# The convolution's input in another order in memory: tile-major, with stepped reads on TensorE

## What is computed

```python
x = x + 0.5 * ffn(layernorm(x))            # ffn: fft over channels, sparse complex weight, ifft, + bias
h = layernorm(layernorm(x), norm1_w, norm1_b)
y = causal_conv_over_time(h, K) + D * h    # K[c, t] = sum_n mix[c, n] * exp(-tau[n] * dt * t)
v = layernorm(x) + y
v = v + gelu(layernorm(v, norm2_w, norm2_b) @ fc1.T + fc1_b) @ fc2.T + fc2_b
x = x + v
x = x + 0.5 * ffn(layernorm(x))
```

## Time and profile before

| | |
|---|---|
| median of 3 runs | 2264.78 us (2264.18 to 2265.57) |
| profiled execution | 2266.64 us, its span 2264.9 us |
| busy share of the span | PE 91%, DVE 59%, ACT 34%, POOL 26% |
| chain that ended last | PE 76%, DVE 8%, POOL 5%, issue 5%, ACT 2% |
| first u written | from 115.6 us |
| first state matmul | 488.51 us |
| MLP's first transposes | 691.82 us |
| largest groups | L1546 678.3 us, L1567 665.6 us (both PE, the MLP) |

### The profile page before, as it was taken

The page is one execution under the profiler, slowest core; times in us unless marked ns, Lnnn a source line. Parts: engine busy times, 40 slices in busy tenths (PEclk is TensorE's granted clock), DMA queues, the critical chain, the costliest instruction groups (busy, mean ns, idle before and its releaser), DMA issues.

```text
span 2264.9 us, 28385 instructions
## 1 busy us (share of the span) xinstructions
PE 2054.4 (91%) x10640; PEld 1034.3 (46%) x10640; DVE 1334.3 (59%) x2099; ACT 766.9 (34%) x939; POOL 596.4 (26%) x416
## 2 busy tenths in 40 slices
PE   7976766639887999999999999999999999999998
PEld 6433323227663444444444444444444444444443
DVE  4899999987787273562726436273562726537242
ACT  1476676756563131221312213031230312213020
POOL 0177777755442021120201102021120211202001
PEclk9988898869897999999999999999999999999999
DMA  6243222138894001101011010101101011010000
GB/s 233 98 177 153 74 88 97 38 88 237 256 274 132 20 30 45 38 19 38 20 56 38 20 38 19 49 28 36 38 19 38 19 56 38 19 38 19 19 19 19
DMA packets 96119, 157.45 MB, mean 70 GB/s; under 512 B 7426, under 2 KB 41730, under 8 KB 95235
## 3 DMA queue, kind: packets, MB, share of 16 engines
q1 hardware_dynamic: 96004, 155.77, 20.9%
HBM read 100.69 MB, written 63.41 MB: 72 GB/s over the span
## 4 chain that ended last, share of the span: by engine, by line
PE 76%; DVE 8%; POOL 5%; issue 5%; ACT 2%; DMA 1%; SPq 1%; DVEq 0%; POOLq 0%; ACTq 0%
PE psum L1546 29%; PE psum L1567 29%; PE psum L1418 9%; PE psum L1410 3%; POOL taps L556 2%; DVE arena L1057 2%; PE psum L1472 2%; POOL taps L553 2%; POOL va L525 1%; ACT arena L704 1%; PE psum L1381 1%; PE psum L1463 1%; DVE ring L1150 1%; PE psum L1392 1%; PE psum L1399 1%
## 5 line engine op out<-in xcount | busy, mean ns | idle before, releaser
L1546 PE MATMUL psum<-arena 128*128 128x512 f16 x3072 | 678.3, 380 | 1.6 <-DVE arena L1267 1.5
L1567 PE MATMUL psum<-arena 128*128 128x512 f16 x3072 | 665.6, 379 | 0.0
L799 ACT ACTIVATE arena<-psum,b1p,sc 128x512 f32<-128x512 f32 x256 | 199.5, 779 | 1037.4 <-PE psum L1546 1037.4
L1567 PEld LDWEIGHTS psum<-arena 128*128 128x128 f16 x3072 | 300.6, 98 | 362.3
L1546 PEld LDWEIGHTS psum<-arena 128*128 128x128 f16 x3072 | 300.9, 98 | 353.4 <-issue 7.5
L525 POOL TENSOR_TENSOR va<-va,mhalf 128x4 f32<-128x4 f32 x80 | 108.8, 1364 | 1295.6 <-DVE va L919 1244.3
L1334 DVE SCALAR_TENSOR_TENSOR arena<-psum,sc,arena 128x512 f32<-128x512 f32 x64 | 48.1, 751 | 579.4 <-PE psum L1567 579.4
L1418 PE MATMUL psum<-m_parts,taps 128*128 128x512 f16 x768 | 211.3, 434 | 95.5 <-DVE taps L1049 79.5
L1311 DVE SCALAR_TENSOR_TENSOR arena<-arena,sc 128x512 f16<-128x512 f32 x256 | 243.8, 952 | 9.1
L1308 DVE TENSOR_SCALAR arena<-arena,sc 128x512 f16<-128x512 f32 x256 | 140.3, 548 | 107.6 <-ACT arena L799 107.3
L1057 DVE TENSOR_TENSOR arena<-taps,arena 128x512 f16<-128x512 f32 (+1 forms) x64 | 166.8, 2608 | 26.8 <-ACT arena L704 26.5
(11 more groups left out here) (157 smaller groups left out, 1844.0 us busy)
## 6 DMA issues: line engine op xcount, KB each, us to landing
arena<-in_x SPq DMA_DIRECT2D x16, 1024.0 KB, 9.9
x_scratch<-arena SPq DMA_DIRECT2D x16, 1024.0 KB, 4.5
taps<-taps_copies SPq DMA_DIRECT2D x64, 256.0 KB, 3.9
y_scratch<-arena SPq DMA_DIRECT2D x32, 512.0 KB, 6.2
arena<-y_scratch SPq DMA_DIRECT2D x15, 1024.0 KB, 7.1
arena<-x_scratch SPq DMA_DIRECT2D x15, 1024.0 KB, 5.5
out<-arena SPq DMA_DIRECT2D x15, 1024.0 KB, 5.1
taps<-taps_copies SPq DMA_DIRECT2D x64, 128.0 KB, 4.6
```

Source lines behind the costliest of these rows:

```text
L799: act.activation(h32[:, hc % 4, :], bank(hc % 2), ACT.Gelu, scale=scale(C_W1), bias=b1p[:, hc:hc + 1])\
L1546: last = pe.matmul(bank(hc % 2), w1_sb[:, a, k, hc * P:(hc + 1) * P], gt[:, b, k, :], start=(n == 0), stop=(n == 3 * KC - 1))
L1567: last = pe.matmul(bank(4 + j % 2), hid[:, a, hc, j * P:(j + 1) * P], w2_sb[:, b, hc, :], start=(n == 0), stop=(n == 3 * HC - 1))
```

## The change

u is laid out as block, tile, part, channel. One tile's 128 channels of a block and a part now lie side by side, 256 bytes; the tiles of one channel lie 256 elements (512 bytes) apart.

- `u_all` is rearranged from `(b t s c)`. L704 and L1057 keep their code; they now write four runs of 128 neighbouring f16, and L1057 reads the high part the same way.
- `inside` reads its 64 columns, one channel of 64 tiles, with a step of 512 bytes.
- `states` takes its 512 columns tile by tile: eight neighbouring channels (16 bytes) of a tile, then the next tile 512 bytes further. The scan still wants the order channel, tile in PSUM, so the matmul writes its bank with a step of 64 columns (256 bytes) inside each run of eight.
- `u_flat` is gone. No instruction is added, taken away or moved on TensorE, ACT, POOL and SP. On VectorE one register instruction per tile (16 per turn of the loop over quads of groups) is added ahead of the low part in the loop.

```diff
-        u_all = area(REG, 4 * REG).bitcast(F16).rearrange("p (b s c t) -> p b s c t", b=BLOCKS, s=2, c=BLK)
-        u_flat = area(REG, 4 * REG).bitcast(F16)
+        u_all = area(REG, 4 * REG).bitcast(F16).rearrange("p (b t s c) -> p b s c t", b=BLOCKS, s=2, c=BLK)
...
             def u_part(o, part, channel, n):

                 blk, place = divmod(o, per_block)
-                at = ((blk * 2 + part) * BLK + place * OC + channel) * TILES
-                return u_flat[:, at:at + n]
+                at = place * OC + channel
+                return u_all[:, blk, part, at:at + n, :]

             def states(o, i):

                 at_least(pe, state_scanned, o - 3)
                 for n, (a, b) in enumerate(PASSES):
-                    last = pe.matmul(bank(i), to_state[:, a, :], u_part(o, b, 0, OC * TILES),
+                    last = pe.matmul(bank(i).rearrange("p (c t) -> p t c", c=OC), to_state[:, a, :],
+                                     u_part(o, b, 0, OC).rearrange("p c t -> p t c"),
                                      start=(n == 0), stop=(n == 2))
                 last.then_inc(state_psum, 1)
...
                 for c in range(OC):
                     for n, (a, b) in enumerate(PASSES):
                         pe.matmul(bank(4 + i)[:, c * TILES:(c + 1) * TILES], taps[:, i, :, a, c],
-                                  u_part(o, b, c, TILES), start=(c == 0 and n == 0), stop=False,
+                                  u_part(o, b, c, 1), start=(c == 0 and n == 0), stop=False,
                                   skip_group_check=True)
```

## The result

The change makes the kernel **0.9% slower**: a median of 2286.01 us (2282.08 to 2290.28, 4 runs) against 2265.18 us in the same measurement, ratio 1.0091 with a 95% interval of 1.0071 to 1.0111. The profiled execution took 2282.08 us, its span is 2280.3; the table sets it against the profiled execution before, 15.4 us shorter.

The account below looks back on a forecast made before the run. VectorE was taken to bound the first stage, TensorE most of the convolution. From 2266.6 us, 83 and 16 less in the first stage and 25 more for state matmuls gave 2192.6, or 2191 against the median; range 2130 to 2305.

Parts of the forecast that it names:

- the price of the single-element reads: Convolution, 24 small matmuls per octet: 35 ns surplus just about covered by 34 ns spare, so nothing added; high end 323 ns.
- rival 1: Convolution, small matmuls: TensorE pays for single-element reads, 2.38 ns per element, 152 ns a matmul; 2315 us, slower; chance 0.17.
- the turn of the sign: Convolution: the change turns slower once an octet grows by 1.87 us in all, from 116 ns a small matmul.
- The state matmuls: Convolution: stepped PSUM write adds 0.36 ns per column, 184 ns a matmul, 0.55 us an octet, 25 us more (0 to 137).
- rival 2: Convolution, state matmuls: the stepped PSUM write costs 2.06 ns per column; 2303 us; chance 0.07.
- the 13 octets: Convolution, where VectorE also splits W2: octets at 3.27 us leave TensorE 0.73 us each, room for the longer state matmuls.
- The first stage: Normalizing tiles and writing u: 83 us less from shorter turns plus 16 less at the last tiles, 99 us less.
- rival 4: First stage, writes of u: the step is not what makes L704 and L1057 slow, so they stay; 2290 us; chance 0.05.
- rival 3: First stage: POOL and VectorE keep holding each other, each L1057 costs 1.95 us, turn 22.0; 2243 us; chance 0.13.
- what is late next: First stage, per turn: TensorE 13.0 us, POOL's large instructions 10.2, ACT's L704 down 7.6, so VectorE stays the limit.
- The MLP: From the MLP on, after the convolution: nothing should differ.
- The 45 octets at TensorE's pace: Convolution: about 45 octets, bound by TensorE at 2.54 us each, would bear the added matmul time in full.

Follow-up runs that it names:

- the order by eights: Against the kernel after: u ordered by group of eight channels, part, tile, channel, so matmuls read columns 16 bytes apart and states write PSUM densely; 2394.0 us.
- the order by fours: Against the kernel after: u ordered by group of four channels, part, tile, channel, so matmuls read columns 8 bytes apart and states write PSUM densely; 2202.1 us.

## Why the prediction was wrong

**The step that failed: the price of the single-element reads.** The forecast was 2191 us, faster; 2286 lies within the stated range, but on the slower side. The prediction took "nothing" for the 24 small matmuls: 64 columns at the surplus of a stepped weight load would cost 35 ns, about the cover of 34. They take 114 to 117 ns, 53 to 56 over the 61. At 1.31 us more per octet (2.77, the mean of both lengths, against 1.46) that is 84 us over 64 octets. Dense columns gave back 89; some 10 of these come from the clock, which fell once in that run in place of nine times, and TensorE was idle again there for 6.8 us. This is rival 1, which had 0.17; it put the turn of the sign at 116 ns a matmul, and the small ones stand about there. Its price, 2.38 ns from ACT's writes, was too high (1.76). The objection to it, that 128 stepped weights fit into 61 ns, is true, for these weights are what fills the 61 ns, but it says nothing of columns: a weight load visits 128 places in 61 ns, where the columns' path needs 1.76 ns for each, 225 in all. A rate seen on one path of TensorE was carried to another.

The Trainium skill, SBUF — State Buffer, Door 1: The DMA port swizzle, was right in direction: accesses that each go to a new 16-byte line are paid for. Its condition that two accesses per line are enough does not hold here: with two, 512 columns took 450 ns, with four 230, dense 213.

**The state matmuls** came close in number, 184 ns more forecast from L1366's 0.36 ns per column and 200 measured (0.39), but by luck. L1366 ran at a granted clock of 0.50 and its surplus was used at full clock as it stood; at half clock a state matmul takes 827 ns (last section) against some 415 for a dense one, 0.80 per column more, so the row was too low by half and the missing conversion made up for it. A dense PSUM write takes the 200 ns back, so the step is the cause, and rival 2, with 2.06 ns per column, fell. PSUM — Partial Sum Buffer, Specifications (TRN2), in the Trainium skill, agrees, and the doubling that was estimated from it (213 more) is nearer than the row of set-up. That eight channels per step are read for nothing held too. What the forecast left out is that VectorE now bounds no octet at all: the 13 octets that were to absorb the state matmuls lost their room of 0.73 us to the small matmuls.

**The first stage** was right in its total, 99 forecast, 92 measured, by two errors that cancel, which is luck. The writes went to 630 and 681 ns, as the dense rows had it, rival 4 fell (its 2290 is the number nearest to the result, by chance), and POOL and VectorE hold each other less than feared (L1056's median is its unhindered time). So the turn is 16.76 us, not 18.4, and rival 3 fell. But the prediction's list of what is late next, TensorE, POOL and ACT, left out SyncE's queue: the loads of x among the taps' copies, 33 us of waits in the first groups. Spreading the copies gave back 31 and 33 us after the change, and next to nothing before it.

**The MLP** did not change, as said. The 45 octets at TensorE's pace became all 64.

The sum as measured: -92 in the first stage; in the convolution +84 for the small matmuls, 0.60 x 64 = +38 for the state matmuls and about 11 for the nine falls of the clock (below), less the 21.2 us that TensorE was idle between 488.5 and 681 us before (busy 171.3 of 192.5) and is not now. That makes 112, against 106.8 measured. The rest was not taken apart; the clock of the kernel before was not at its full level throughout either (mean 0.95 over these 192.5 us, 0.93 after).

## What to carry to other kernels

An operand that is cheap to write and one that is cheap to read for matmuls may be the same tensor in different orders; count for each reader how many 16-byte places it visits per column, and look for an order that gives both sides a short run (here two channels: 4-byte runs to write, four columns per place to read). A rate seen on one port, weight loads or another engine's writes, is no price for another port; where a read repeats 1536 times, bound it from above and let that bound weigh. And when a stage gets a third shorter, look at what its DMA queue does in the same order, not only at its engines.

## What was not expected of the hardware

- The price of a read place is a time (it stays at either clock), while the price of the PSUM step goes with the clock. In the kernel after, the granted clock fell nine times during the convolution for some 2.5 us, with TensorE busy throughout. The timeline shows one, and the windows row its mean clock of 0.57:

```profile
424.35 0.94 PE L1481 MATMUL psum<-state_parts,from_state 128*128 128x512 f16 x2
425.08 2.77 PE L1462 MATMUL psum<-arena,to_state 128*128 128x512 f16 x3
427.56 2.99 PE L1472 MATMUL psum<-arena,taps 128*128 128x64 f16 x24
430.38 0.61 PE L1481 MATMUL psum<-state_parts,from_state 128*128 128x512 f16 x2
430.83 1.45 PE L1462 MATMUL psum<-arena,to_state 128*128 128x512 f16 x3
...
424.00:428.00 4.00, 4.00 (x14) 1.68 (x13) 0.03 (x1) 1.58 (x2) 0.58 (x1) 0.57 0.32 87
429.00:505.00 76.00, 76.00 (x496) 57.57 (x495) 33.00 (x36) 26.27 (x34) 24.09 (x17) 1.00 0.43 121
```

  The three state matmuls take 2.48 us instead of 1.24, double, at the 1.2 GHz level. At half clock through the whole convolution the order by eights read its places at 1.76 ns, the same as the order by fours at full clock. Nine falls at 1.24 us are about 11 us. What brings them on is open: in the one run with dense weights none of the convolution's state matmuls was at half clock after the first four octets, in the one with dense columns one octet was.
- In the order by eights TensorE was busy for 190 of 190 us and had a granted clock of 0.50 over all of them. The clock had fallen while TensorE waited for the last tiles (376 to 396 us, mean 0.58) and did not rise once its slow-reading matmuls ran, one right behind the other. In the kernel after it rose again from the same start.
- A write of single f16, 128 bytes apart, cost ACT and VectorE 5.0 to 5.1 ns per element; written in pairs, 512 bytes apart, the same 512 elements took 657 and 739 ns, nearly what they take in runs of 128 (630 and 681).
